# A graph-network kernel: the second message matrix folded into the update's, degrees counted in an attention pass, the update's base made ahead, and four smaller moves

## The chip, the cores and the metric

One core of one Trainium2 chip runs the whole program in one launch. The metric is the device time of an execution in microseconds (us); lower is better. TensorE is written PE, VectorE DVE, ScalarE ACT, GpSimd POOL and SyncE SP, as in the profile.

## The reference

`x` is 6250 nodes by 128; 100000 edges sorted by destination carry `src`, `dst`, 64 attributes and a weight. Every layer works on `h = relu(layernorm(x))` and adds its result to `x`.

```python
# layer 0: messages from col to row, then an MLP and a batch norm with fixed statistics
agg = segment_sum(h[col] * fsum[:, None], row)
out = softplus(agg @ Wi1 + bi1) @ Wi2 + bi2
out = gamma * (out - mov_mean) * rsqrt(mov_var + BN_EPS) + beta
# layer 1: attention with one head, twice, each followed by a residual and a layer norm
# layer 2
messages = relu(concat(x[src], edge_attr, g) @ Wm1.T + bm1) @ Wm2.T + bm2
aggregated = segment_sum(messages, dst) / maximum(degree, 1)[:, None]
delta = relu(concat(x, aggregated, g) @ Wu1.T + bu1) @ Wu2.T + bu2
out = layernorm(x + delta) * ln_g + ln_b
# layer 3: attention with 8 heads, self loops included, plus a bias
```

## The kernel before

Nodes lie in 52 tiles of 128 (`NBP`), in 13 groups of 4 (`NG`, `GN`). X, ACC, H, XI and Y hold one row per node, in SBUF. Edges lie in 832 tiles of 128 slots, worked in 104 halves of 8 tiles; `edge_records`, `onehots`, `onehots_turned` and `layer0_messages` are DRAM tensors.

**Setup** (`setup`). DVE finds the slot of each edge in 7 chunks of 112 columns. Each chunk runs `slot_round` for 25 pairs of node tiles: `equal_to`, four scans in `running_count`, `carry_on`, `mask`, `gather_slots` (L661 to L676). All of them read and write SBUF. POOL shares the first chunk. From chunk 0 on, POOL scatters the records of the finished chunks to DRAM with one indirect DMA per column (L439, 782 in all), while DVE works on the next chunk.

**Layer 0** has a pass by destination (`layer0_dst_pass`) and one by source (`layer0_src_pass`). In the latter POOL subtracts an index row from the messages' indices (L1342), ACT makes a one-hot of the difference with Abs and Relu (L1352, L1354), PE multiplies (`sum_tiles`, L1116) and DVE adds the 8 products to the node tiles (`add_sums`, L1129), whose places it first loads into registers (`node_tiles`, L1089). Rings of 4 one-hots and 8 message buffers tie them together. `softplus_product` follows; its `after0` multiplies by `bn_scale` (L1787), adds to X (L1788) and counts statistics (L179).

**A node product** (`node_product`) goes through the 13 groups: ACT normalises 4 tiles into XI (L1741), PE turns them (L896), ACT copies them out of PSUM (L947), PE multiplies (L922), DVE takes the result (`take_product`), SP stores the table. With two sources and `w2` it is the update of layer 2: PE turns both (L896), adds both products in PSUM (L905), ACT applies Relu (L960), PE multiplies by `wu2T` (L920), DVE adds `bu2` (L1861), adds XI (L1862) and counts statistics (L1864).

**Attention** (`gat_pass`): POOL gathers rows with 832 indirect DMAs (L1389), PE picks and sums, DVE adds sums. Before the first gather POOL reduces a maximum over partitions (L1481). `mlp_pass` is layer 2's pass over edges; it sums relu(...) rows with a column of ones, the degree. Then `degree2` divides (L1841 to L1844), a node product with `wm2T` gives the mean message (L1849, L1854), and the update follows. `norm_into_x` normalises and adds into X.

All engines meet at the end of each block. The order within a block is written by hand and held by semaphores; each engine runs its own list in order.

## Time and profile before

| what | us |
|---|---|
| median of 3 runs | 7350.69 (7348.01 to 7358.4) |
| profiled execution, its own time | 7349.52 |
| its span | 7347.5 |

| stretch | us | PE busy | DVE busy | ACT busy | POOL busy | PE clock |
|---|---|---|---|---|---|---|
| setup, 0 to 1252 | 1252 | 107 | 777 | 160 | 848 | 0.58 |
| layer 0 by destination, to 2349 | 1097 | 507 | 332 | 220 | 809 | 0.66 |
| layer 0 by source, to 2623 | 274 | 215 | 188 | 238 | 199 | 0.98 |
| softplus product, first table, to 2744 | 121 | 71 | 75 | 58 | 0 | 0.72 |
| attention pass 0, to 3804 | 1060 | 502 | 347 | 297 | 786 | 0.58 |
| second table, to 3876 | 72 | 23 | 58 | 30 | 0 | 0.71 |
| attention pass 1, to 4928 | 1052 | 500 | 355 | 297 | 785 | 0.59 |
| norms and layer 2's table, to 5022 | 94 | 22 | 68 | 49 | 0 | 0.64 |
| layer 2 over edges, to 6075 | 1053 | 805 | 380 | 239 | 785 | 0.68 |
| layer 2's update, norm, layer 3's table, to 6234 | 159 | 96 | 107 | 76 | 0 | 0.82 |
| attention pass with 8 heads, to 7322 | 1088 | 491 | 528 | 73 | 787 | 0.66 |
| last rows and store | 25.5 | 0 | 18 | 0 | 0 | 0.50 |

Busy times are those of the profiled execution; an engine's sum is below the span because it waits. The clock is the granted share of 2.4 GHz, a mean over the stretch: 0.50 is 1.2 GHz throughout. Register and semaphore instructions and the issue of DMAs are not busy time, except POOL's indirect DMAs, whose rows are the time POOL makes descriptors.

### The profile page before, as it was taken

What the parts mean: (1) busy time and instruction counts of PE and PEld (TensorE: products, weight loads), DVE (VectorE), ACT (ScalarE), POOL (GpSimd) and SP (SyncE); (2) the same over time, 40 slices, a digit from 0 to 9 for tenths busy, and PEclk for the clock granted to TensorE, in tenths of its full rate; (3) what the DMA queues carried; (4) which work ended last, traced back from release to release, by engine and by line L of the source; (5) the groups of instructions that cost most, each with busy time, mean ns of one, the idle gap of its engine ahead of it and who ended that gap; (6) DMA issues with size and microseconds to landing.
All of it is one profiled execution on the core that took longest, in us unless ns stands there. A gap on an engine that the chain in (4) does not pass through costs nothing. (4 is left out here: it accounts for less than half of the span.)

```text
span 7347.5 us, 89302 instructions
## 1 busy us (share of the span) xinstructions
PE 3339.2 (45%) x17325; PEld 2965.8 (40%) x17326; DVE 3231.2 (44%) x10135; ACT 1737.8 (24%) x4276; POOL 4999.3 (68%) x5176
## 2 busy tenths in 40 slices
PE   5000000444444854444444444436777775444443
PEld 2000000444444744444433444435767674344443
DVE  8777711322333663333344333344333336544445
ACT  7000000222123852222232222223222224000000
POOL 2777776777777717777746777754777770777775
PEclk9555555666666975555556565556666667666666
DMA  6233332444444624444424444433444441444443
GB/s 230 92 111 104 105 118 85 160 155 155 156 157 146 211 65 136 130 134 130 130 84 140 131 133 131 130 91 117 136 134 134 135 124 34 133 133 132 132 131 106
DMA packets 507457, 942.53 MB, mean 128 GB/s; under 512 B 204299, under 2 KB 240635, under 8 KB 507256
## 3 DMA queue, kind: packets, MB, share of 16 engines
q1 hardware_dynamic: 349240, 637.41, 26.1%
q0 software_dynamic: 158144, 304.31, 15.9%
q8 instruction: 26, 0.43, 0.0%
q14 instruction: 47, 0.39, 0.0%
HBM read 673.90 MB, written 270.84 MB: 129 GB/s over the span
## 5 line engine op out<-in xcount | busy, mean ns | idle before, releaser
L1389 POOL DMA_INDIRECT edge_buf<-node_table,ixr x1664 | 1571.8, 945 | 618.8 <-issue 507.0
L1389 POOL DMA_INDIRECT Y<-node_table,ixr x1664 | 1569.6, 943 | 519.3 <-issue 518.4
L1129 DVE TENSOR_TENSOR ACC<-ACC,bank 128x129 f32 (+2 forms) x3744 | 1090.6, 291 | 1096.3 <-PE bank L1116 468.4
L1556 PE MATMUL bank<-adc,turned_buf 128*128 x2496 | 340.2, 195 | 1476.7 <-issue 591.5
L1297 POOL DMA_INDIRECT layer_messages<-edge_buf,ixr x832 | 809.3, 973 | 291.4 <-issue 263.3
L439 POOL DMA_INDIRECT edge_records<-edge_buf x782 | 790.7, 1011 | 255.1 <-issue 246.9
L1556 PEld LDWEIGHTS bank<-adc,turned_buf 128*128 128x128 bf16 x2496 | 257.1, 103 | 1606.2 <-issue 1552.1
L1116 PE MATMUL bank<-edge_buf,Y 128*128 128x129 f32 (+2 forms) x3744 | 821.9, 406 | 143.3 <-ACT edge_buf L1542 98.8
L1116 PE MATMUL bank<-Y 128*128 128x129 f32 (+1 forms) x3328 | 770.1, 423 | 160.4 <-ACT Y L1542 91.5
L1116 PEld LDWEIGHTS bank<-edge_buf,Y 128*128 128x128 f32 x3744 | 765.3, 309 | 174.1 <-DVE ACC L1129 136.9
L1116 PEld LDWEIGHTS bank<-Y 128*128 128x128 f32 x3328 | 720.0, 325 | 183.6 <-issue 87.7
L1504 DVE TENSOR_REDUCE pk<-bank 128x16 f32<-128x48 f32 (+1 forms) x312 | 100.2, 321 | 1006.9 <-DMA Y<-node_table,ixr 505.3
L1245 PE MATMUL bank<-ident,Y 128*128 128x128 f32 x832 | 204.3, 427 | 729.7 <-DVE Y L1082 727.4
L1245 PEld LDWEIGHTS bank<-ident,Y 128*128 128x128 f32 x832 | 163.2, 223 | 752.7 <-issue 563.4
L1675 PE MATMUL bank<-wmbT,turned_buf 64*128 64x128 f32 x1664 | 287.0, 340 | 181.1 <-DVE edge_buf L1614 90.7
L1675 PEld LDWEIGHTS bank<-wmbT,turned_buf 64*128 64x128 f32 x1664 | 260.5, 243 | 214.4 <-issue 200.3
L488 PE MATMUL bank<-Y,H 128*128 128x2 f32 (+1 forms) x6 | 1.4, 358 | 740.0 <-DVEq L735 740.0
L1257 PE MATMUL bank<-H,Y 128*128 x1664 | 323.8, 377 | 2.6 <-DVEq L1207 2.6
L1257 PEld LDWEIGHTS bank<-H,Y 128*128 128x128 f32 x1664 | 323.2, 297 | 2.8 <-issue 2.8
L1285 ACT COPY Y<-bank 128x512 f32<-128x512 f32 x208 | 123.8, 595 | 840.5 <-PE bank L1257 840.1
L1195 DVE COPY edge_buf<-XI 128x8 f32 (+1 forms) x104 | 18.4, 177 | 664.6 <-DMA layer_messages<-edge_buf,ixr 664.6
L488 PEld LDWEIGHTS bank<-Y,H 128*128 128x128 f32 x6 | 1.4, 325 | 740.2 <-issue 740.2
(284 smaller groups left out, 5309.1 us busy)
## 6 DMA issues: line engine op xcount, KB each, us to landing
Y<-onehots SPq DMA_DIRECT2D x416, 512.0 KB, 3.7
turned_buf<-onehots_turned SPq DMA_DIRECT2D x312, 256.0 KB
edge_buf<-edge_records SPq DMA_DIRECT2D x208, 288.0 KB, 2.9
layer_messages<-ACC SPq DMA_DIRECT2D x26, 2112.0 KB
onehots<-Y SPq DMA_DIRECT2D x104, 512.0 KB, 2.6
XI<-layer_messages SPq DMA_DIRECT2D x78, 528.0 KB, 4.4
edge_records<-XI SPq DMA_DIRECT2D x1, 29952.0 KB
onehots_turned<-turned_buf SPq DMA_DIRECT2D x104, 256.0 KB
```

The costliest lines, as they stand in the source:

```text
L439: pool.indirect_dma_start(rec_d, bass.IndirectOffsetOnAxis(ap=ixs[h][:, j:j + 1], axis=0), rec[h][:, j, :], None, bounds_check=SLOTS - 1, ...
L1116: ins = nc.tensor.matmul(places.at(q, j, w), tiles_of_half(onehots)[:, j, :], messages[:, j, 0:w], start=True, stop=True)
L1129: nc.vector.tensor_tensor(acc, acc, places.at(q, j, w), ALU.add).then_inc(added, 1)
L1195: nc.vector.tensor_copy(rows[h][:, :, D:D + 1], fields[:, bass.ds(t, G), R_SLOC - EA:R_SLOC - EA + 1]) \
L1245: ins = nc.tensor.transpose(bank[j // 4][:, (j % 4) * P:(j % 4) * P + P], tiles_of_half(oh[h])[:, j, :], ident[:, :])
L1257: ins = nc.tensor.matmul(bank[2 + j // 4][:, (j % 4) * P:(j % 4) * P + P], ohT[h][:, j * P:j * P + P], Hflat[:, bass.ds(at[j] * AW, D)], s ...
L1285: nc.scalar.copy(ohT[h][:, at], bank[n][:, :]).then_inc(ohT_ready, 1)
L1297: pool.indirect_dma_start(msg_d, bass.IndirectOffsetOnAxis(ap=ixr[h][:, j:j + 1], axis=0), rows[h][:, j, 0:MW], None, bounds_check=SLOTS - ...
L1389: pool.indirect_dma_start(ring[q][:, j, 0:w], None, table, bass.IndirectOffsetOnAxis(ap=ixr[q][:, j:j + 1], axis=0)).then_inc(rows_in[q], 16)
L1504: st.then(nc.vector.tensor_reduce(ps, picks(q).rearrange("p (j t k) -> p j k t", j=G, t=3), AX.X, ALU.add))
L1556: ins = nc.tensor.matmul(picks(q)[:, j * 6 * heads:(j + 1) * 6 * heads], ohbT[q][:, j * P:j * P + P], adc[:, bass.ds(at[j] * (6 * heads), ...
L1675: ins = nc.tensor.matmul(bank[2 + j // 4][:, (j % 4) * P:(j % 4) * P + P], attrT[q % 2][:, j * P:j * P + P], wmbT[:, :], start=True, stop= ...
```

## The change

1. **Layer 2.** `wm2T` is folded: setup multiplies `wubT` with `wm2` into `wmuT`, and `bm2` into the row `cmu_row`. Degrees are counted in attention pass 1: a column of ones in each buffer makes its sums 130 wide; `end1` derives `inv_deg` and `has_edge` there. `has_edge` is turned to a row, out to DRAM and back to one partition of Y (`flag_row`) within `norm_into_x`. The node product of layer 2's table gets a second product per group, `Base`: `wuaT` on the same turned rows plus `cmu_row` times the flags, which DVE takes into H with `cu_col`. The table is built in ACC. `beside2` adds `bu2` to XI. `degree2` and the product with `wm2T` are gone; `update_product` replaces the two-source one.
2. **Copies on DVE.** Node products that normalise on ACT and have no `before` (three of four) copy their turned tiles on DVE.
3. **Setup's counts in PSUM.** In chunks 1 to 6 the running counts lie in PSUM banks 2 and 3, and the scans' second operand, which they bypass, in bank 1.
4. **Layer 0 by source.** Places are loaded for two halves at a time; every eighth one-hot is made by DVE in one instruction; POOL runs one reduction over partitions at the end of its list there.
5. `bn_scale` is multiplied into `Wi2` in setup; `after0` adds straight to X.

```diff
+            cums_psum = [bank[2 + h][:, 0:2 * CH].rearrange("p (q c) -> p q c", q=2) for h in range(2)]
+            unread = bank[1][:, 0:CH]
...
-                                    work(h, eqs[h], cums[h], bass.ds(i * 2 + h, 1))
+                                    work(h, eqs[h], running[h], bass.ds(i * 2 + h, 1))
...
-                                    v.tensor_tensor_scan(cum[:, q, :], eq[:, q, :], eq[:, q, :], offs[0:EP, q, b],
-                                                         ALU.add, ALU.bypass).then_inc(count, 1)
+                                    v.tensor_tensor_scan(cum[:, q, :], eq[:, q, :], eq[:, q, :] if helped else unread,
+                                                         offs[0:EP, q, b], ALU.add, ALU.bypass).then_inc(count, 1)
...
+                        nc.tensor.matmul(bank[6][:, P:2 * P], wm2, wubT[:, :], start=True, stop=True)
+                        nc.tensor.matmul(bank[7][0:1, P:2 * P], bm2_col[:, :], wubT[:, :], start=True, stop=True)
...
+            dve_copies = normed is not None and before is None
...
+                        if dve_copies and g + 1 < NG:
+                            copy(g + 1)
                         take_product(dve, v, then, g, prod, taken, cols, after)
+                        if second:
+                            dve.wait_ge(second_done, g + 1)
+                            second.take(v, g).then_inc(second_taken, 1)
...
+        def update_product(src, w1, base, w2, before, after):
...
+                    def add_base(g):
+                        dve.wait_ge(in_hid, g + 1)
+                        v.tensor_tensor(of_group(g), of_group(g), bank[2 + g % 2][:, :], ALU.add).then_inc(z_ready, 1)
+                    prepare(0)
+                    prepare(1)
+                    add_base(0)
+                    for g in range(NG):
+                        if g + 2 < NG:
+                            prepare(g + 2)
                         if g + 1 < NG:
-                            copy(g + 1)
+                            add_base(g + 1)
+                        take_product(dve, v, then, g, prod, taken, D, after)
...
-                tiles[0:1, bass.ds(n * G, G)], engines=[engine], min_val=0,
+                tiles[0:1, bass.ds(n * G, halves * G)], engines=[engine], min_val=0,
...
+                    nc.gpsimd.memset(gmax[:, :], 0.0).then_inc(gmax_set, 1)
+                    pool.wait_ge(gmax_set, 1)
+                    pool.partition_all_reduce(gmax_all[:, :], gmax[:, :], P, bass.bass_isa.ReduceOp.max).then_inc(gmax_set, 1)
+                    pool.wait_ge(gmax_set, 2)
...
+                    def onehot_here(i, q):
+
+                        dve.wait_ge(msg_in[q], i * 16 + 16)
+                        dve.wait_ge(summed, i * deep + q - oh_deep + 1)
+                        nc.vector.tensor_tensor(tiles_of_half(onehots[q]), bank[0][:, 0:P].unsqueeze(1).to_broadcast([P, G, P]),
+                                                by_tile[q][:, :, D:D + 1].to_broadcast([P, G, P]), ALU.is_equal) \
+                            .then_inc(oh_ready[q], 1)
+
+                    def body(i, first):
+                        for pair in range(deep // 2):
+                            n = i * deep + 2 * pair
+                            at = node_tiles(mybir.EngineType.DVE, acc_of_s, n, 2)
+                            for k in range(2):
+                                add_to(dve, n + k, 2 * pair + k, two_sets, sums, at[k * G:k * G + G], D, summed, n + k + 1, added)
+                            if 2 * pair + 1 == by_vector - oh_deep:
+                                onehot_here(i, by_vector)
...
-                then(v.tensor_tensor(ACC[:, at, 0:D], rows_psum, columns(bn_scale, 2), ALU.mult))
-                then(v.tensor_tensor(X[:, at, :], X[:, at, :], ACC[:, at, 0:D], ALU.add))
+                then(v.tensor_tensor(X[:, at, :], X[:, at, :], rows_psum, ALU.add))
...
+                    if l == 1:
+                        deg = ACC[:, :, D + 1:D + 2]
+                        then(v.tensor_scalar(inv_deg[:, :].unsqueeze(2), deg, 1.0, None, ALU.max))
+                        then(v.reciprocal(inv_deg[:, :], inv_deg[:, :]))
+                        then(v.tensor_tensor(has_edge[:, :].unsqueeze(2), deg, inv_deg[:, :].unsqueeze(2), ALU.mult))
...
+                def product(g, turned):
+                    o = bank[2 + g % 2][:, :]
+                    nc.tensor.matmul(o, wuaT[:, :], turned, start=True, stop=False)
+                    return nc.tensor.matmul(o, cmu_row[:, :], flag_row[:, Base.at(g)], start=False, stop=True)
...
-            node_product([XI], [wmaT], after_h, normed=relu_norm_x, store=(tab_d[2], H, D))
+            node_product(XI, wmaT, after_h, normed=relu_norm_x, store=(tab_d[2], ACC, D), second=Base)
...
+                add_row(v, then, XI, vec["L2_gnn_bu2"][0])
...
-                then(v.tensor_tensor(ACC[:, at, 0:D], rows_psum, columns(vec["L2_gnn_bu2"][0], 2), ALU.add))
-                then(v.tensor_tensor(H[:, at, 0:D], ACC[:, at, 0:D], XI[:, at, :], ALU.add))
+                then(v.tensor_tensor(Y[:, at, :], rows_psum, XI[:, at, :], ALU.add))
...
-            node_product([XI, Y], [wuaT, wubT], after_u, w2=wu2T, bias=cu_col)
+            update_product(ACC, wmuT, update_base, wu2T, mean2, after_u)
```

PE's list where layer 2's table is made, from its first group on, before and now: `wmaT` makes the table, `ident` turns.

```order
L896 MATMUL bank<-ident,XI 128x128 x8
L922 MATMUL bank<-wmaT,edge_buf 128x128 x4
L896 MATMUL bank<-ident,XI 128x128 x4
L922 MATMUL bank<-wmaT,edge_buf 128x128 x4
L896 MATMUL bank<-ident,XI 128x128 x4
```

```order
L912 MATMUL bank<-ident,XI 128x128 x8
L1979 MATMUL bank<-edge_buf,wuaT 128x512
L1980 MATMUL bank<-Y,cmu_row 128x512
L926 MATMUL bank<-wmaT,edge_buf 128x128 x4
L912 MATMUL bank<-ident,XI 128x128 x4
```

Two products of 512 columns now stand ahead of the table's four in each of the 13 groups.

PE's list in layer 2's update, before (its first group and most of the second) and now.

```order
L896 MATMUL bank<-ident,XI 128x128 x4
L896 MATMUL bank<-ident,Y 128x128 x4
L905 MATMUL bank<-edge_buf,wuaT 128x512
L905 MATMUL bank<-edge_buf,wubT 128x512
L896 MATMUL bank<-ident,XI 128x128 x4
L896 MATMUL bank<-ident,Y 128x128 x4
L920 MATMUL bank<-wu2T,edge_buf 128x128 x4
```

```order
L993 MATMUL bank<-ident,ACC 128x128 x8
L1000 MATMUL bank<-edge_buf,wmuT 128x512
L993 MATMUL bank<-ident,ACC 128x128 x4
L1000 MATMUL bank<-edge_buf,wmuT 128x512
L1007 MATMUL bank<-wu2T,edge_buf 128x128 x4
L993 MATMUL bank<-ident,ACC 128x128 x4
```

Per group four turns and one product of 512 columns went, and the product for the next group now stands ahead of the last four.

POOL's list between the pass by source and the first attention pass, before and now; the bare ISA row loads the code that the reduction needs.

```order
L1342 TENSOR_TENSOR Y<-iota_row,edge_buf 128x1024
L88 REGISTER_ALU
L88 COMPARE_AND_BRANCH
L1318 UNCONDITIONAL_BRANCH
L105 ISA
L1478 UNCONDITIONAL_BRANCH
L1481 ISA
L1481 ISA gmax_all<-gmax 128x1
L1389 DMA edge_buf<-node_table,ixr_115 128x129 x8
```

```order
L1432 MEMSET gmax 128x8
L1434 ISA
L1434 ISA gmax_all<-gmax 128x8
L1404 UNCONDITIONAL_BRANCH
L105 ISA
L1585 UNCONDITIONAL_BRANCH
L1588 ISA gmax_all<-gmax 128x1
L1496 DMA edge_buf<-node_table,ixr_118 128x129 x8
```

The bare ISA row moved from the start of the attention pass to the end of the pass by source.

## Rows read from the trace of the kernel before

**Rows 1.** The page, part 1: busy time, share of the span, instructions.
```profile
PE 3339.2 (45%) x17325; PEld 2965.8 (40%) x17326; DVE 3231.2 (44%) x10135; ACT 1737.8 (24%) x4276; POOL 4999.3 (68%) x5176
```
**Rows 2.** The page, part 5: groups; busy us, mean ns, idle before, releaser.
```profile
L1389 POOL DMA_INDIRECT Y<-node_table,ixr x1664 | 1569.6, 943 | 519.3 <-issue 518.4
L1297 POOL DMA_INDIRECT layer_messages<-edge_buf,ixr x832 | 809.3, 973 | 291.4 <-issue 263.3
```
**Rows 3.** Stretches: length, busy us (count) of each engine, PE clock, DMA share.
```profile
204.00:928.00 724.00, 0.00 (x0) 0.00 (x0) 566.89 (x1875) 13.63 (x76) 553.56 (x542) 0.50 0.33 108
...
2351.00:2623.00 272.00, 215.43 (x1664) 196.15 (x1664) 185.77 (x833) 237.76 (x208) 198.78 (x104) 0.98 0.65 204
2667.00:2706.00 39.00, 22.99 (x91) 19.77 (x89) 34.98 (x105) 0.00 (x0) 0.00 (x0) 0.50 0.00 0
...
4990.00:5020.00 30.00, 22.20 (x156) 19.21 (x156) 11.04 (x26) 26.45 (x65) 0.00 (x0) 0.89 0.34 100
...
6109.00:6162.00 53.00, 49.32 (x253) 33.10 (x252) 34.47 (x104) 21.23 (x39) 0.00 (x0) 0.97 0.00 1
```
**Rows 4.** Groups, POOL, 204 to 928 us (DVE counts slots beside it).
```profile
L439 POOL DMA_INDIRECT edge_records<-edge_buf x542 | 554.3, 1023 | 179.0 <-issue 174.5 <-DMA edge_buf<-in_edge_attr_dram 4.6
```
**Rows 5.** Timeline, setup: start us, us, engine, line.
```profile
401.37 0.39 DVE L673 TENSOR_TENSOR XI<-XI,Y 128x224 f32<-128x224 f32 x1
401.46 1.14 POOL L439 DMA_INDIRECT edge_records<-edge_buf  x1 [0.30 <-issue]
...
402.20 0.82 DVE L676 TENSOR_TENSOR XI<-XI 128x224 f32 x2
402.91 0.97 POOL L439 DMA_INDIRECT edge_records<-edge_buf  x1 [0.30 <-issue]
```
**Rows 6.** Groups, DVE alone, 2359 to 2623 us (layer 0 by source).
```profile
L1129 DVE TENSOR_TENSOR ACC<-ACC,bank 128x128 f32 x416 | 119.7, 288 | 86.0 <-DVE H L1129 66.3 <-issue 13.8 <-PE bank L1116 5.9
```
**Rows 7.** Line L1089: duration ns min/median/max, first and last start.
```profile
L1089 DVEq TENSOR_LOAD <-acc_of_s x104: 593/598/850, 2354.8 to 2620.2; - x104
```
**Rows 8.** Groups, whole span: a one-hot on DVE.
```profile
L1082 DVE TENSOR_TENSOR Y<-bank,XI 128x1024 f32<-128x1024 f32 x104 | 127.3, 1224 | 11.8 <-DVE XI L1183 9.9
```
**Rows 9.** Timeline, start of attention pass 0 and of pass 1.
```profile
2752.02 0.38 POOL L1481 PARTITION_ALL_REDUCE gmax_all<-gmax  x1 [139.93 <-issue]
...
3876.04 0.39 POOL L1481 PARTITION_ALL_REDUCE gmax_all<-gmax  x1 [84.96 <-DVEq L1429]
```
**Rows 10.** Groups, 2667 to 2706 us (`after0`).
```profile
L1788 DVE TENSOR_TENSOR X<-X,ACC 128x256 f32<-128x256 f32 x26 | 11.0, 425 | 0.9
L1787 DVE TENSOR_TENSOR ACC<-bank,bn_scale 128x256 f32<-128x256 f32 x26 | 11.0, 424 | 2.2
```
**Rows 11.** Groups, 4990 to 5020 us (layer 2's table).
```profile
L1741 ACT ACTIVATE XI<-X,shift,var 128x128 f32<-128x128 f32 x52 | 21.5, 501 | 2.0 <-PEq L106 2.0
...
L947 ACT COPY edge_buf<-bank 128x512 f32<-128x512 f32 x13 | 7.6, 584 | 0.3 <-PE bank L896 0.3
```
**Rows 12.** Timeline, one group of layer 2's update, PE at full clock.
```profile
6133.59 1.09 PE L905 MATMUL bank<-edge_buf,wuaT 128*128 128x512 f32 x2
6133.80 0.42 DVE L1862 TENSOR_TENSOR H<-ACC,XI 128x256 f32<-128x256 f32 x1
6134.26 0.49 DVE L1864 BATCH_NORM_STATS2 stats<-H 128x6 f32<-128x128 f32 x2
6134.78 0.42 DVE L1861 TENSOR_TENSOR ACC<-bank,L_gnn_bu 128x256 f32<-128x256 f32 x1
6135.38 0.60 PE L896 MATMUL bank<-ident,XI 128*128 128x128 f32 x4
6136.32 1.05 PE L920 MATMUL bank<-wu2T,edge_buf 128*128 128x128 f32 x7
```
**Rows 13.** Groups: 128x512 on DVE, out of SBUF (`mean2`) and out of PSUM.
```profile
L1849 DVE TENSOR_TENSOR ACC<-ACC,mean 128x512 f32<-128x512 f32 x13 | 9.0, 691 | 2.3 <-DVE Y L1854 1.4 <-PEq L788 0.5
...
L990 DVE TENSOR_SCALAR XI<-bank,bi_col 128x512 f32<-128x512 f32 x13 | 9.8, 751 | 6.7 <-PE bank L1019 6.0
```

More of the change, by code:

```diff
@@ L928, in _ @@
                     for g in range(NG):
-                        if w2 is not None:
-                            first(g)
                         if g + 1 < NG:
@@ L951, in _ @@
                             normed(g).then_inc(norm_done, 1)
-                    copy(0)
+                    if not dve_copies:
+                        copy(0)
                     for g in range(NG):
@@ L1316, in layer0_src_pass @@
             rounds = HALVES // deep
+            by_vector = deep - 1
             with nc.Block() as block:
@@ L1705, in after, with add_row @@
                 then(v.tensor_copy(ad[:, at, :], rows_psum[:, :, D + heads:cols]))
-            node_product([XI], [wx[l]], after, before, normed, cols=cols, store=(table, H, D + heads))
-        def add_row_to_x(v, then, row):
+            node_product(XI, wx[l], after, before, normed, cols=cols, store=(table, H, D + heads))
+        def add_row(v, then, t, row):
             in_psum = bank[7][:, 0:D]
             then(v.tensor_copy(in_psum, row[:, :]))
-            then(v.tensor_tensor(X[:, :, :], X[:, :, :], per_col(in_psum), ALU.add))
+            then(v.tensor_tensor(t[:, :, :], t[:, :, :], per_col(in_psum), ALU.add))
         def self_loops(v, then, heads):
```

263 lines of the change are left out of this document (168 added, 95 removed).

## The prediction

> **What bounds the kernel.** I read the page's first part for the engines, its groups for the costliest work, then stretches, and inside each stretch the groups, the releasers and a piece of timeline. POOL is busy 68% of the span, more than any other [rows 1], and its indirect DMAs go at a fixed pace: 943 ns for a gather, 973 ns for a scatter, with 0.3 us between two that nobody but POOL's own issue fills [rows 2, 5]. Six long stretches (setup's scatter, layer 0 by destination, three attention passes, layer 2 over edges) are such lists. There DVE, ACT and PE may gain or lose a little and nothing moves. The change leaves the number of gathers and scatters as it is. What it can win lies in the pace of setup's scatter, in the start of attention pass 0, and in the short stretches where POOL isn't the bound: layer 0 by source and the node products.
>
> **The change, term by term.**
>
> *Counts in PSUM (setup).* From 204 to 928 us DVE counts slots while POOL scatters. POOL's 542 scatters there take 1023 ns each [rows 4], those of layer 0, beside other DVE work, 973 [rows 2]. The timeline shows why: the scatter at 401.46 begins while `mask`, which reads two SBUF tensors, is running, and takes 1.14 us; it ends later by what `mask` had left. The scatter at 402.91 begins behind the last `gather_slots` by start and takes 0.97 [rows 5]. So a scatter waits where a DVE instruction with two SBUF inputs is already under way. The change gives the scans, `mask` and `gather_slots` one SBUF input each. In the stretches of layer 0 DVE's instructions are of that kind, and the pace there is the floor. Gain: 542 x (1023 - 973) = 27 us; I take 26, as a few instructions with two SBUF inputs stay in `slot_rows`. POOL must stay the bound for that. DVE needs 724 / 6 = 121 us per chunk [rows 3]; POOL's 112 scatters need 112 x (0.973 + 0.30) = 143 us, and 148 now. DVE has 22 us to spare. Setup's additions (two small products, two copies, one multiply) lie before the scatter's end and cost nothing while it lasts.
>
> Against this stands a rule. The rows show no price for PSUM: 424 ns out of PSUM, 425 ns out of SBUF for 128x256 [rows 10]. The Trainium skill (VectorE: DVE Perf Modes, the section on the TRN2 errata) gives VectorE a fixed 58 cycles out of SBUF and 120 out of PSUM, 0.065 us more at 0.96 GHz. By it, as an estimate, the 250 instructions of a chunk that touch the counts would add 16 us, DVE would stand at 137 us, and the sum would be the same with 6 us of margin left.
>
> *Layer 0 by source.* In 272 us DVE is busy 186 and idle 86 [rows 3, 6]; ACT is busy 238, PE 215, POOL 199. The idle time isn't a lack of work: before each half DVE's sequencer loads eight places, 598 ns [rows 7], and cannot issue an add meanwhile. That is 104 times about 0.73 us with what stands around it. DVE is the bound, ACT is next. Now 52 loads of sixteen places take their place. If a load is a fixed price, 52 x (0.73 - 0.09) = 33 us go; the 0.09 is the register work that stays between two halves. DVE gets 13 one-hots of 1.22 us [rows 8], each hiding the load behind it, so 13 x (1.22 + 0.06 - 0.73) = 7 us come back. Gain 26 us. The others then need, of (272 - 26) / 13 = 18.9 us per eight halves: ACT 7/8 x 238 / 13 = 16.0, PE 16.6, POOL 13.4. None is the new bound, but ACT is near. What I don't have is the price of sixteen places. Its bounds: 0.6 us (nothing per place) and 1.2 us (twice eight). I take 0.6, since 0.6 for one place or eight is what a round trip looks like, and keep 1.2 as a rival.
>
> *The reduction's code.* Pass 0 begins at 2744, and its reduction starts at 2752.02, behind nothing but POOL's own issue; pass 1 begins at 3876, and its reduction starts at 3876.04 [rows 9]. The two stretches differ by the same 8 us (1060 and 1052 in the table of stretches). Now the load stands at the end of POOL's list by source. POOL's last one-hot there ends about 10 us before DVE's last add (four halves of 2.6 us, the depth of the ring), and load and reduction take 8. Gain 8 us; if the cover is short, the next block starts some us later and the gain shrinks.
>
> *`after0`.* 26 times one instruction of 424 ns and the 0.03 us to the next. DVE is busy 35 of 39 us [rows 3, 10]. Gain 26 x 0.458 = 12 us. PE at half clock is busy 23 of the 27 us that stay, so it isn't the bound.
>
> *Copies on DVE.* ACT has 21.5 us of norms and 7.6 of copies in 30 [rows 3, 11]. Without copies it needs 1.65 us per group; the group takes 26.45 / 13 = 2.03 us now [rows 3]. DVE with its copy of about 0.7 [rows 13] and two takes of about 0.55 (0.42 and a short copy, an estimate from rows 12) needs about 1.85. Two tables gain 2.4 and 1.2 us, 3.5 together.
>
> *Degrees.* Three small instructions in `end1`, +1 us. Columns 130 instead of 129 and the memsets lie beside POOL's gathers. The flags' way through DRAM lies beside 13 groups of norm work. `add_row` on XI (7 us on DVE) lies beside POOL's first four halves of gathers, 32 x 1.25 = 40 us, which need nothing of DVE. All cost nothing as long as POOL is the bound there.
>
> *The base, made ahead.* Layer 2's table took 30 us, bound by ACT. PE now has per group four turns, eight short and four long matrix instructions. From one group of the old update: four long ones take 6135.38 - 6133.59 = 1.79 us, eight turns 0.94, eight short ones about 1.0 [rows 12]. That is 0.47 + 1.0 + 1.79 = 3.25 us, against ACT's 1.65 and DVE's 0.7 + 2 x 0.46 + 0.75 = 2.4. PE is the bound: 13 x 3.25 = 42, and 4 to fill and empty. Cost 46 - 30 = +16 us.
>
> *The update.* From the end of layer 2's edges at 6075 to 6162 us stand `degree2`, the product with `wm2T` and the update, 87 us; the update is bound by PE, busy 49 of 53 [rows 3]. Now DVE has per group `mean2` 0.69 with 0.15 around it, the base 0.72, and two takes of 0.46 + 0.52 [rows 12, 13]: 3.55 us, against PE's 0.47 + 0.90 + 1.0 = 2.4. DVE is the bound: 13 x 3.55 = 46, and 5 for the chain of the first group, where PE still has half clock. 51 instead of 87: gain 35 us (36 less the add's wait).
>
> **Sum.** -26 - 26 - 8 - 12 - 3.5 + 1 + 16 - 35 = -93.5 us. The profiled execution took 7349.5 (its span 7347.5 and 2.0 around it), so 7256; the median of the runs is 1.2 above it: 7257 us.
>
> **Rivals.**
> *A load of sixteen costs twice that of eight.* 39 of 52 loads are not hidden: 39 x 0.6 = 23 us come back, total 7280. For it: nothing in the trace has another size. The Trainium skill has both answers. DMA: Bandwidth & Descriptors (Latency and other measured facts) calls 600 ns a floor of the load, which speaks for my price; Runtime: NRT & Kernel Launch (Instruction fetch mechanics) gives about 200 ns per register from HBM. By the second, eight would take 1.6 us; the trace's 0.6 denies it here. Chance 0.15.
> *Setup's scatter isn't freed* because something else of DVE (its writes, or the comparison in SBUF) delays it: 26 us stay, 7283. Against it stands layer 0's pace. Chance 0.10.
> *PE stays at half clock* in the two rebuilt stretches, as it did all through `after0` at 0.50 [rows 3]. Then the table needs 13 x 6.5 + 4 = 89 us and the update 13 x 4.7 + 5 = 66, 58 us more: 7315. Against it: the old table and update, with PE less or as busy, ran at 0.89 and 0.97. Chance 0.06.
> *The first two together*, 7306: 0.02.
> *Slower than before*: DVE becomes setup's bound. If the counts in PSUM made each of a chunk's 250 instructions slower, DVE would pass POOL at 22 / 250 = 0.09 us each. From there every further us of a chunk counts six times. The kernel is slower by over 0.2% when 67.5 us of other gains and 15 more are eaten, 83 / 6 = 14 us per chunk above the 148 of now, which is 41 us in all or 0.165 us per instruction; total 7366 and up. Against it: 424 beside 425 ns [rows 10]. For it: no row has a scan in PSUM. Chance 0.03.
> The forecast keeps 0.64.
>
> **Numbers.** My case alone spans 7240 (every term at its full size, a smaller fill) to 7273 (ACT eats a part by source, PE fills slowly). The first two rivals at 7280 and 7283 must be in, with their own spread: 7238 to 7292. That leaves out the third to fifth rival, 0.11, and some 0.05 of the tails. 0.2%, 15 us, is what a measurement can tell from no change. Every case but the last is faster by more: faster 0.96, same 0.01, slower 0.03.
>
> **What would show it.** Right: scatters in setup at 973 ns beside DVE, setup shorter by about 26 us; layer 0 by source near 246 us with loads near 0.6 us; no wait of 8 us at the first reduction; layer 2's table at 46 us with PE without a gap; the update at 51 us with DVE without a gap. Wrong: loads of 1.2 us, or DVE idle on one-hots of ACT; scatters still at 1023 ns; PE's clock near 0.5 in the table or the update; DVE chunks over 143 us.

## The result, and the profile after

The changed kernel takes 7312.08 us (7307.35 to 7317.1, five runs) where before takes 7350.69 (7346.68 to 7358.4, five runs): ratio 0.9948, 95% interval 0.9933 to 0.9962. The sign is the forecast's, the size is not: 38.6 us gained instead of 93.5, and the time lies above the range of 7238 to 7292. The profiled executions differ by 32.1 us of span (7347.5 and 7315.4); the profiled one after is the slowest of its five. What follows is between these two.

Stretches of the changed kernel, cut at the events that cut the table of before. Columns: length, busy us and count of PE, PEld, DVE, ACT, POOL, PE's clock, DMA share, GB/s; the last three lines are pieces of layer 2's table and of `after0`.

```profile
0.00:1225.40 1225.40, 113.05 (x298) 51.43 (x299) 782.56 (x2480) 160.58 (x360) 821.42 (x909) 0.58 0.37 122
1225.40:2320.90 1095.50, 511.75 (x2496) 487.89 (x2496) 331.53 (x632) 219.60 (x417) 809.30 (x832) 0.66 0.44 151
2320.90:2587.00 266.10, 201.75 (x1664) 191.93 (x1664) 204.10 (x848) 204.51 (x182) 172.80 (x93) 0.98 0.67 211
...
6051.00:6128.50 77.50, 48.10 (x182) 32.94 (x182) 41.17 (x104) 16.99 (x26) 0.00 (x0) 0.74 0.00 1
...
2631.00:2658.00 27.00, 15.43 (x89) 13.28 (x88) 23.68 (x79) 0.00 (x0) 0.00 (x0) 0.82 0.00 0
...
4938.00:4961.00 23.00, 22.02 (x57) 12.60 (x58) 6.88 (x13) 18.96 (x50) 0.00 (x0) 0.50 0.08 23
4961.00:4996.50 35.50, 33.51 (x152) 18.15 (x151) 21.86 (x40) 0.00 (x0) 0.00 (x0) 1.00 0.26 78
```

They answer to [rows 3]. Stage by stage, forecast and measured:

| term | forecast | measured |
|---|---|---|
| setup | -26 | -27 (1252 to 1225) |
| layer 0 by source | -26 | -8 (274 to 266) |
| the reduction's code | -8 | -7 (pass 0: 1060 to 1053) |
| `after0` | -12 | -12 (39 to 27) |
| copies on DVE | -3.5 | -1 (table 0 in 28.5, was 28.8; layer 3's table in 26.8, was 27.4) |
| degrees | +1 | +1 |
| the base made ahead | +16 | +31 (layer 2's table 27 to 58; the forecast counted the old one as 30) |
| the update | -35 | -10 (87 to 77) |

Layer 0 by destination gives 1 us, and the 8-head pass takes 2 us more, a spread that the experiments show between equal programs too. With these the column adds up to -32, as the span says. Three terms carry the error: 18 us by source, 15 in layer 2's table, 25 in the update.

**By source**, the loads of places on the line of the loads (duration ns, least, median, largest; first and last start):

```profile
L1168 DVEq TENSOR_LOAD <-acc_of_d x416: 593/598/633, 2719.1 to 7280.7; - x139
...
L1168 DVEq TENSOR_LOAD <-acc_of_s x52: 1096/1100/1359, 2327.1 to 2581.7; - x52
```

A load of eight takes 598 ns as in [rows 7], one of sixteen 1100. The timeline shows what it costs where no one-hot covers it, and where one does:

```profile
2450.32 0.29 DVE L1211 TENSOR_TENSOR ACC<-ACC,bank 128x128 f32 x1 [1.66 <-issue]
...
2453.54 0.29 DVE L1211 TENSOR_TENSOR H<-H,bank 128x128 f32 x1
2455.07 0.29 DVE L1211 TENSOR_TENSOR ACC<-ACC,bank 128x128 f32 x1 [1.24 <-PE bank L1195]
...
2458.30 0.29 DVE L1211 TENSOR_TENSOR H<-H,bank 128x128 f32 x1
2458.58 1.22 DVE L1460 TENSOR_TENSOR Y<-bank,edge_buf 128x1024 f32<-128x1024 f32 x1
...
2460.11 0.29 DVE L1211 TENSOR_TENSOR ACC<-ACC,bank 128x128 f32 x1 [0.30 <-issue]
```

DVE idles 1.66 us before the add that follows an open load where its list starts another turn of the loop, and 1.24 us at most of the others. The profile names PE's product there, but that had ended at 2454.18, while the load ran from 2453.67 to 2454.77. With a one-hot, DVE's last add ends at 2458.59 and the next begins at 2460.11, 1.52 us later: the one-hot hides the load, but takes longer than most of the gaps that it fills, and saves nothing.

**Layer 2's table** runs at half clock until 4961, though PE is busy without a gap from 4942 on. One group at half clock, and one at full:

```profile
4947.58 1.92 PE L1979 MATMUL bank<-edge_buf,wuaT 128*128 128x512 f32 x2
4949.42 2.07 PE L1980 MATMUL bank<-Y,cmu_row 1*128 1x512 f32 x2
4951.42 2.08 PE L926 MATMUL bank<-wmaT,edge_buf 128*128 128x128 f32 x8
4953.29 1.06 PE L912 MATMUL bank<-ident,XI 128*128 128x128 f32 x4
...
4964.29 1.02 PE L1979 MATMUL bank<-edge_buf,wuaT 128*128 128x512 f32 x2
4965.24 1.12 PE L1980 MATMUL bank<-Y,cmu_row 1*128 1x512 f32 x2
4966.29 1.16 PE L926 MATMUL bank<-wmaT,edge_buf 128*128 128x128 f32 x8
4967.29 0.60 PE L912 MATMUL bank<-ident,XI 128*128 128x128 f32 x4
```

A group takes 4954.14 - 4947.58 = 6.56 us at half clock (the next L1979 begins at 4954.14) and 4967.73 - 4964.29 = 3.44 at full. Three groups fall in the slow part: about 3 x 3.1 = 9 us, and more with the start.

**The update**: one group of the changed kernel.

```profile
6099.96 0.69 DVE L1995 TENSOR_TENSOR ACC<-ACC,inv_deg 128x512 f32<-128x512 f32 x1 [0.15 <-DVE stats L183]
6100.76 0.50 PEld L993 LDWEIGHTS bank<-ident,ACC 128*128 128x128 f32 x4 [2.66 <-DVEq L971]
6100.76 0.90 PE L993 MATMUL bank<-ident,ACC 128*128 128x128 f32 x4 [2.47 <-DVEq L971]
...
6101.45 1.92 PE L1000 MATMUL bank<-edge_buf,wmuT 128*128 128x512 f32 x2
...
6103.41 0.69 DVE L975 TENSOR_TENSOR H<-H,bank 128x512 f32<-128x512 f32 x1 [2.76 <-PE bank L1000]
...
6104.26 0.42 DVE L2000 TENSOR_TENSOR Y<-bank,XI 128x256 f32<-128x256 f32 x1 [0.17 <-PE bank L1007]
```

Read it as a ring. DVE scales group g+2 (L1995); PE turns it (L993), since its list has these turns ahead of the first product of g+1 (L1000); DVE's add of the base (L975) waits 2.76 us for that product; then come the takes of g, and PE waits 2.47 us for the next scaling. DVE and PE work in turns, 6.3 us a group, and neither is the bound. The clock, in the same place:

```profile
6093.50:6097.50 4.00, 3.25 (x9) 2.22 (x10) 1.03 (x2) 0.59 (x1) 0.00 (x0) 0.59 0.00 0
6097.50:6101.00 3.50, 1.03 (x8) 0.84 (x8) 2.81 (x8) 0.72 (x1) 0.00 (x0) 0.98 0.00 0
6101.00:6104.50 3.50, 3.50 (x13) 2.47 (x12) 0.93 (x2) 0.96 (x2) 0.00 (x0) 0.51 0.00 0
```

It is full while PE mostly waits (busy 1.03 of 3.5 us) and half while PE works. The Trainium skill (TensorE: Matmul & The Clock Gate, the section on how the clock gate's oscillation bites in real kernels) describes work in bursts, with waits for DMA between, that meets the low clock each time; the trace shows the same with waits for DVE.

### The profile page after: what moved, and what is told of

It reads as the page before. It is cut to its first block and busy times, and to the rows that moved or that the text cites. A ratio compares the mean times of both kernels' runs of the same rounds, so it can differ in the third digit from the quotient of the medians.

```text
span 7315.4 us, 88637 instructions
## 1 busy us (share of the span) xinstructions
PE 3315.1 (45%) x17147; PEld 2929.7 (40%) x17148; DVE 3264.7 (45%) x10122; ACT 1673.6 (23%) x4184; POOL 4946.4 (68%) x5165
## 5 line engine op out<-in xcount | busy, mean ns | idle before, releaser
L1211 DVE TENSOR_TENSOR ACC<-ACC,bank 128x129 f32 (+3 forms) x3744 | 1091.4, 291 | 1077.1 <-PE bank L1195 502.4
L445 POOL DMA_INDIRECT edge_records<-edge_buf x782 | 763.7, 977 | 255.3 <-issue 243.5
L1195 PE MATMUL bank<-edge_buf,Y 128*128 128x129 f32 (+3 forms) x3744 | 812.9, 404 | 150.1 <-ACT edge_buf L1649 98.6
L1195 PE MATMUL bank<-Y 128*128 128x129 f32 (+2 forms) x3328 | 759.4, 418 | 164.3 <-ACT Y L1649 91.8
```

Source lines behind the costliest of these rows:

```text
L445: pool.indirect_dma_start(rec_d, bass.IndirectOffsetOnAxis(ap=ixs[h][:, j:j + 1], axis=0), rec[h][:, j, :], None, bounds_check=SLOTS - 1, ...
L1195: ins = nc.tensor.matmul(places.at(q, j, w), tiles_of_half(onehots)[:, j, :], messages[:, j, 0:w], start=True, stop=True)
L1211: nc.vector.tensor_tensor(acc, acc, places.at(q, j, w), ALU.add).then_inc(added, 1)
```

## The experiments

Each is an edit of the changed kernel. For the tables and the update the times are from the first turn or the last add before it to the last take; the changed kernel itself has 56.4 us for layer 2's table and 77.0 for the update.

**1. The order of the update.**

```diff
                     for g in range(NG):
+                        if g + 1 < NG:
+                            first(g + 1)
                         if g + 2 < NG:
                             turn(g + 2)
-                        if g + 1 < NG:
-                            first(g + 1)
                         last(g)
```

> Only the order of PE's work in the update is other: each group's first product is issued ahead of the turns of the group behind it. Theory A (in the changed kernel DVE and PE wait for each other in a ring: take, scale, turn, first product, add; 6.3 us per group): now the add of the base needs nothing of the group just scaled, DVE's own 3.55 us per group is the bound, the update takes 13 x 3.55 + 5 = 51 us instead of 77.5, and the kernel gains 26 us, to about 7286. Theory B (the loss is PE's clock alone, which each burst of the changed kernel meets at its lower level): the order changes nothing that matters, the first product stays at 1.9 us and the update within 5 us of 77.

Measured: 7294.22 us (7290.9 to 7294.83, four runs), ratio to before 0.9921 (0.9905 to 0.9938). The update takes 54.0 us (6052.1 to 6106.1), 23 less; 51 and a gain of 26 were expected. By the medians the kernel gains 18 us on the changed one, by the spans of the profiled executions 23: that of the changed kernel is the slowest of its five.

```profile
6080.07 1.07 PE L1000 MATMUL bank<-edge_buf,wmuT 128*128 128x512 f32 x2
...
6081.90 0.69 DVE L1995 TENSOR_TENSOR ACC<-ACC,inv_deg 128x512 f32<-128x512 f32 x1 [0.15 <-DVE stats L183]
...
6082.74 0.69 DVE L975 TENSOR_TENSOR H<-H,bank 128x512 f32<-128x512 f32 x1
...
6083.20 1.06 PE L1007 MATMUL bank<-wu2T,edge_buf 128*128 128x128 f32 x8
...
6083.85 0.42 DVE L2000 TENSOR_TENSOR Y<-bank,XI 128x256 f32<-128x256 f32 x1 [0.42 <-PE bank L1007]
```

The first product is done before DVE scales, and the add of the base follows at once. A group takes 4.03 us (one first product at 6080.07, the next at 6084.10). The clock is 0.99 from 6058 on, although nothing was done for it: it rose with the ring cut. Theory A, then. How much of the 23 us is the ring's and how much the clock's, the run doesn't part. The 0.42 us left in front of the take is the same fault once more: the last product stands behind turns that wait for the scaling. Experiment 8 moves them too.

**2. The table without the one-row product.**

```diff
-                    nc.tensor.matmul(o, wuaT[:, :], turned, start=True, stop=False)
-                    return nc.tensor.matmul(o, cmu_row[:, :], flag_row[:, Base.at(g)], start=False, stop=True)
+                    return nc.tensor.matmul(o, wuaT[:, :], turned, start=True, stop=True)
```

> The one-row product (weights 1x128, flags 1x512) is left out of layer 2's table, and with it the term of bm2 for nodes that have an edge. A group then needs 3.44 - 1.12 = 2.32 us of PE at full clock and 6.57 - 2.0 = 4.6 at half. Theory A (the one-row product is also what keeps PE at half clock for the table's first 22 us, though PE is busy without a gap there): the clock rises within 6 us of the first turn, as in the other tables, and the table takes 1 x 4.6 + 12 x 2.32 + 3 = 36 us instead of 58. Theory B (the rise comes late for another reason, such as the length of the pause before): half clock for 22 us again, 4.6 groups in it, then 8.4 x 2.32, with 2 to empty: 44 us.

Measured, in one execution: the table takes 33.4 us (4940.3 to 4973.7).

```profile
4940.00:4945.50 5.50, 4.80 (x16) 3.37 (x16) 1.38 (x2) 5.50 (x15) 0.00 (x0) 0.50 0.00 0
4945.50:4974.00 28.50, 27.40 (x168) 20.85 (x167) 25.72 (x50) 13.20 (x35) 0.00 (x0) 0.99 0.37 111
```

The clock is up 5 us after the first turn instead of 22. Of the 23 us, 13 x 1.12 = 15 are the product's own time at full clock; the rest is the earlier rise. Theory A, as far as it goes: this run changes the product's length and its rows at once.

**3. The same product on all rows.** Rows or length?

```diff
-                    return nc.tensor.matmul(o, cmu_row[:, :], flag_row[:, Base.at(g)], start=False, stop=True)
+                    return nc.tensor.matmul(o, wubT[:, :], turned, start=False, stop=True)
```

> In layer 2's table the one-row product is replaced by a product of the same shape at PE's output, 128x512 fp32, but with all 128 rows of weights and data (wubT and the turned nodes; the base is then another number than the reference's). PE's time stays the same: 6.57 us per group at half clock, 3.44 at full. Theory A (a product that fills one row of PE hardly counts as work for the clock): the clock rises within 6 us of the first turn, and the table takes 1 x 6.57 + 12 x 3.44 + 3 = 51 us instead of 56.4. Theory B (the late rise has to do with long products, or with the start of this stretch): half clock for 22 us again, 56 us.

Measured, in one execution: 43.0 us (4943.1 to 4986.1).

```profile
4943.00:4949.00 6.00, 5.45 (x18) 3.42 (x19) 1.38 (x2) 6.00 (x17) 0.00 (x0) 0.60 0.00 0
4949.00:4987.00 38.00, 36.58 (x193) 24.91 (x191) 27.35 (x50) 12.53 (x33) 0.00 (x0) 1.00 0.28 83
```

Same amount of output, and the clock is up after 5 us: theory A. With the product's time kept, it was its single row that held the clock down. It is also shorter than I expected (51). A group at full clock takes 4964.97 - 4961.92 = 3.05 us, not 3.44, and the weight loads come earlier. Ahead of this product and ahead of L926 PEld idles 0.24 us, ahead of the one-row product, and of the one behind it, 0.76:

```profile
4962.35 0.19 PEld L1980 LDWEIGHTS bank<-edge_buf,wubT 128*128 128x128 f32 x1 [0.24 <-issue]
```

and in the changed kernel

```profile
4965.24 0.29 PEld L1980 LDWEIGHTS bank<-Y,cmu_row 1*128 1x128 f32 x2 [0.76 <-issue]
```

**4. The clock warmed up ahead of the table.** Twelve, then eighteen products of 128x512 in the norms before it, unread; all else as in the changed kernel. The edit with twelve:

```diff
+                        pe.wait_ge(norm_done, 9)
+                        for n in range(12):
+                            nc.tensor.matmul(bank[6][:, :], ident[:, :], ACC[:, 0:GN, 0:D], start=True, stop=True)
```

> PE gets 12 products of 128x512 fp32, whose result nobody reads, in the last 15 us of the norms ahead of layer 2's table; all else as in the changed kernel. Theory A (only the cold start costs): the clock is at its upper level at the first turn and stays there, and the table takes 13 x 3.44 + 2 = 47 us instead of 58. Theory B (the one-row product pulls the clock down): the clock falls to 0.50 again in the first groups and the table takes 53 us or more.

Measured, in one execution: 53.3 us (4940.8 to 4994.1). The clock was full from 4923, PE idle from 4931, the clock half at 4938, and it came back at about 4956. So the run doesn't tell the theories apart; the level was lost before the table began.

> As warm_table, with 18 unread products instead of 12, so that PE works up to the table's start; in warm_table they ended at 4931, the clock fell at about 4937, and the first turn at 4941 met half clock. The one-row product stays. Theory A (the one-row product holds the clock down whatever stood before it): the clock is full at the first turn, falls to 0.50 within the first two groups, and the table still takes 50 us or more from the first turn to the last take. Theory B (only the start decides): full clock throughout, 13 x 3.44 = 45 us.

Measured, in one execution: 50.1 us (4941.0 to 4991.1). PE ended at about 4936.3.

```profile
4937.00:4939.00 2.00, 0.00 (x0) 0.00 (x0) 0.69 (x2) 0.28 (x1) 0.00 (x0) 1.00 0.00 0
4939.00:4941.00 2.00, 0.00 (x1) 0.01 (x1) 0.00 (x0) 1.71 (x5) 0.00 (x0) 0.73 0.00 0
4941.00:4950.00 9.00, 8.58 (x24) 5.17 (x25) 2.23 (x4) 9.00 (x24) 0.00 (x0) 0.50 0.00 0
4950.00:4992.00 42.00, 40.61 (x185) 22.22 (x184) 26.47 (x48) 9.40 (x25) 0.00 (x0) 1.00 0.26 76
```

The level was lost in the pause of 4.7 us between the last unread product and the first turn. Again neither theory is met at the first turn. What the runs add is that with the one-row product the rise is not only late but varies, also where nothing near the table was changed. From the first turn to the rise it is 22 us in the changed kernel, update_order (experiment 1) and loads_small (experiment 6), and the table takes 56.4 or 56.5 us; it is 16 us in hot_back (experiment 7) and in the two runs on setup's scatters, counts_sbuf and scan_sbuf, and the table takes 53.3. The warm_table run, with 15.9 and 53.3, is one of these, so its unread products gained nothing that shows. Only warm_long, with 9 and 50.1, is quicker, and one run can't tell whether the warming did it. All eight runs with the one-row fp32 product took 9 us or more, the five without it (no_flags, full_rows, flags_bf16 and the two of experiment 8) 4 to 6.

**5. The flags in bf16.** The bias row is cut in three bf16 parts that add up to it; one pass of three rows takes the place of the fp32 product.

```diff
-    flag_d = dram("edge_flags", [NBP, P])
+    flag_d = dram("edge_flags", [NBP, P], BF16)
...
-                    return nc.tensor.matmul(o, cmu_row[:, :], flag_row[:, Base.at(g)], start=False, stop=True)
+                    return nc.tensor.matmul(o, cmu_rows[:, :], flag_row[:, Base.at(g)], start=False, stop=True)
```

> The one-row fp32 product of layer 2's table becomes one of three rows in bf16 (the row of Wm2's bias cut in three bf16 parts that add up to it, the flags 0 or 1 three times), one pass in place of fp32's. By the run without the product the table takes 33.4 us from the first turn to the last take, with it 56.4. Theory A (its time and its hold on the clock both go by how long it runs): about a quarter of 1.12 us per group, clock up within 8 us, the table at 33.4 + 13 x 0.3 = 37 us, the kernel 19 us faster than the changed one. Theory B (any product of few rows keeps the clock down): half clock for 20 us or more, 45 us or more.

Measured: 7301.74 us (7300.58 to 7303.13, four runs), ratio to before 0.993 (0.9914 to 0.9947). The table takes 38.2 us (4944.0 to 4982.2), 18 less than in the changed kernel and 15 less than in the three runs that had 53.3. The kernel gains 10 us by the medians, 13 by the ratios to before, where 19 were expected. The timeline has the new product at

```profile
4975.23 0.39 PE L1996 MATMUL bank<-Y,cmu_rows 3*128 3x512 bf16 x1
```

and the stretches up to and from the clock's rise:

```profile
4943.90:4949.00 5.10, 4.60 (x15) 2.55 (x16) 1.38 (x2) 5.10 (x15) 0.00 (x0) 0.59 0.00 0
4949.00:4983.00 34.00, 32.67 (x182) 20.66 (x181) 27.26 (x50) 13.39 (x35) 0.00 (x0) 1.00 0.31 93
```

Theory A: 0.39 us instead of 1.12, and the clock is up after 4 us, though three rows are few too. A product of few rows need not hold the clock down, then, where it is short. Cutting the row in parts on DVE put 0.3 us in front of the table (66.3 us from attention pass 1's last add to the first turn, 66.0 in the changed kernel); in experiment 8 that is done in setup.

**6. Loads of other sizes, by source.** Per pair of halves 4 + 4 and 2 + 6 places. `some_tiles` is a load of `count` places from `at` on.

```diff
-                            at = node_tiles(mybir.EngineType.DVE, acc_of_s, n, 2)
-                            for k in range(2):
-                                add_to(dve, n + k, 2 * pair + k, two_sets, sums, at[k * G:k * G + G], D, summed, n + k + 1, added)
+                            for k, first_load in enumerate((4, 2)):
+                                at = list(some_tiles(acc_of_s, (n + k) * G, first_load))
+                                at += list(some_tiles(acc_of_s, (n + k) * G + first_load, G - first_load))
+                                add_to(dve, n + k, 2 * pair + k, two_sets, sums, at, D, summed, n + k + 1, added)
```

> Layer 0 by source, DVE's loads of places: per pair of halves 4 + 4 and 2 + 6 places in four loads instead of one of sixteen; nothing else. Theory A (about 0.1 us per load and 0.063 per place, drawn from 598 ns for eight and 1100 for sixteen): 0.22, 0.35, 0.47 us for 2, 4 and 6 places, together 1.4 us per pair instead of 1.1, and with a little for each more issue the stretch takes some 10 to 20 us more than 266. Theory B (0.6 us is a floor up to eight places): all four 0.6, 2.4 us per pair, the stretch 50 us longer.

Measured, in one execution: 7414.37 us; the adds by source take 354.0 us (2333.0 to 2687.0) where the changed kernel's take 254.5, 99 more. One load of four, one of two, one of six:

```profile
L1175 DVEq TENSOR_LOAD <-acc_of_s x1: 341/341/341, 2433.3 to 2433.3; - x1
...
L1175 DVEq TENSOR_LOAD <-acc_of_s x1: 534/534/534, 2435.6 to 2435.6; - x1
...
L1175 DVEq TENSOR_LOAD <-acc_of_s x1: 1408/1408/1408, 2436.3 to 2436.3; - x1
```

Four, eight and sixteen places take 341, 598 and 1100 ns: (1100 - 598) / 8 = 0.063 us per place and about 0.09 fixed. There is no floor at 0.6, and theory B falls. But two and six take 534 and 1408: (1408 - 534) / 4 = 0.22 us per place. I expected neither. These two pay about 3.5 times as much per place. Neither count is a multiple of four; the load of six also starts two places past one, and no run here parts count and start, but the load of two starts where others do. The Trainium skill has both numbers: DMA: Bandwidth & Descriptors (Latency and other measured facts) gives 600 ns as a floor, which the 341 ns here denies; Runtime: NRT & Kernel Launch (Instruction fetch mechanics) gives some 200 ns per register, which is near the 0.22 us between two and six places and not near four, eight or sixteen. The sum fits: 341 + 341 + 534 + 1408 = 2.62 us a pair and three more issues at some 0.1, less 1.10, is 1.8 us, and 52 x 1.8 = 94.

**7. DVE's one-hots given back.**

```diff
-            by_vector = deep - 1
+            by_vector = deep
...
-                            if 2 * pair + 1 == by_vector - oh_deep:
-                                onehot_here(i, by_vector)
```

> Layer 0 by source with DVE's 13 one-hots given back to POOL and ACT; loads stay at sixteen places. Theory A (DVE stays the bound; its one-hot stands where a visible load of 1.10 us would stand, and the step between two pairs takes 1.52 us with it and 1.66 without): the stretch grows by 13 x 0.14 = 2 us at most, ACT's 104 x 2.3 = 239 us being still below 266. Theory B (ACT was the bound of the old stretch, and freeing it brought the 8 us that were gained): the stretch returns to 274 us.

Measured, in one execution: the adds take 252.5 us (2333.1 to 2585.6), 2 less than with them. DVE is the bound either way, and its one-hots earn nothing. Theory A, with the sign of the 2 us turned: the expectation took 1.66 us for every step without a one-hot, but where the one-hots stood DVE now idles 1.33 us (as before 2460.09), against 1.52 with them, and 13 x 0.19 = 2.5.

**Setup's scatters**, two runs. First the counts back in SBUF, the scans' unread second input staying in PSUM:

```diff
-                            running = cums if helped else cums_psum
+                            running = cums
```

> DVE's running counts in setup go back from PSUM to SBUF, nothing else. Theory A (a scatter waits where a DVE instruction that reads two SBUF tensors is under way): the scatters beside them take 1023 ns again instead of 972, and setup is 26 to 28 us longer. Theory B (the scatters got shorter for another reason, such as the unread second input of the scans): they stay near 975 ns and setup within 5 us.

Then the other way round:

```diff
-                                    v.tensor_tensor_scan(cum[:, q, :], eq[:, q, :], eq[:, q, :] if helped else unread,
+                                    v.tensor_tensor_scan(cum[:, q, :], eq[:, q, :], eq[:, q, :],
```

> Counts stay in PSUM; only the scans' second input, which they don't use, is the comparison in SBUF again in place of a row in PSUM. With the counts back in SBUF the scatters stayed at 975 ns, against what was expected: none of the 150 that began while a scan ran was delayed, and the 52 that began while the mask ran found only 0.12 us of it left. Theory A (a scatter waits for what is left of any DVE instruction with two SBUF inputs, and the scans were the ones that mattered once the two lists had fallen into step): the scatters that begin in a scan's first half take 1.05 to 1.12 us again, the mean is 985 ns or more, and setup grows by 5 us or more. Theory B (scans never delayed a scatter, the mask and the order of the lists do): 972 to 976 ns and no change.

Measured, one execution each, POOL's scatters from 206 to 928 us (busy, mean ns, idle before), first with the counts in SBUF, then with the scans' second input in SBUF:

```profile
L445 POOL DMA_INDIRECT edge_records<-edge_buf x560 | 545.8, 975 | 176.6 <-issue 168.7 <-DMA edge_buf<-in_edge_attr_dram 7.9
```

```profile
L445 POOL DMA_INDIRECT edge_records<-edge_buf x553 | 548.6, 992 | 174.2 <-issue 166.0 <-DMA edge_buf<-in_edge_attr_dram 8.2
```

The first result goes against what I expected (1023): with the scans' second input in PSUM, moving the counts back costs nothing that shows. The second meets theory A: 86 of the 156 scatters that began while a scan ran took over 1050 ns, the mean is 992, and the first add by source comes 10 us later than in the other runs of that chip (2345.0 against 2334.3). In before, all but one of the 77 scatters that began in a mask and 75 of the 148 that began in a scan were over 1050 ns. In the run with counts in SBUF the mask still reads two SBUF tensors and 52 scatters began in it; only 2 were over 1050, since most found no more than 0.14 us of it left, where those of before found 0.30. Both lists repeat themselves, so they fall into step, and the step decides what a scatter meets. The Trainium skill (SBUF — State Buffer, SBUF: two separate sides) calls the port that VectorE and GpSimd share an exclusive lock that an instruction with two SBUF inputs holds to its end; the runs agree with that, and show besides that the sum of such instructions says little. The mean was 1023 ns in before, 992 with the counts alone in PSUM, 975 with the scans' second input alone in PSUM and 972 with both: the second alone wins nearly all of the 27 us, the first alone some 17 of them, and they don't add up.

**8. The edits that helped, together.** PE's order `first(g + 1)`, `last(g)`, `turn(g + 2)`; the flags in bf16, the parts made in setup; the one-hots given back.

```diff
...
+                        if g + 1 < NG:
+                            first(g + 1)
+                        last(g)
                         if g + 2 < NG:
                             turn(g + 2)
-                        if g + 1 < NG:
-                            first(g + 1)
-                        last(g)
...
```

> Three edits together: in the update PE issues the first product of the next group, then the last product of this one, then the turns; layer 2's table has the flags' product in bf16 with three rows (the parts of the bias row made in setup); DVE's one-hots by source go back to POOL and ACT. If they add up: update 13 x 3.6 + 5 = 52 us instead of 77 (in update_order, where the last product still stood behind the turns, 54), table 38 instead of 56, by source 2 less. Sum -25 - 18 - 2 = -45 to the changed kernel, about 7267 where before takes 7350. The other way (the edits meet in the same wait, or the flags' three more transfers delay the table): 7285 or more.

Measured: 7267.8 us (7267.38 to 7268.89, four runs) where before has 7350.13 in the same comparison: ratio 0.9888 (0.9871 to 0.9904). The update takes 48.5 us (6032.6 to 6081.1), the table 38.7 (4938.0 to 4976.7), the adds by source 252.3: 28.5, 17.7 and 2.2 less than in the changed kernel, 48.4 in sum, and the spans differ by 7315.4 - 7266.9 = 48.5. By the medians it is 44 us less than the changed kernel, of 45 expected. The edits add up. DVE in the update:

```profile
6049.82 0.69 DVE L983 TENSOR_TENSOR H<-H,bank 128x512 f32<-128x512 f32 x1
...
6050.43 0.42 DVE L2009 TENSOR_TENSOR Y<-bank,XI 128x256 f32<-128x256 f32 x1
...
6053.34 0.69 DVE L983 TENSOR_TENSOR H<-H,bank 128x512 f32<-128x512 f32 x1
```

3.52 us per group (6049.82 to 6053.34), against the 3.55 that the prediction had for DVE as the bound.

> best3 with the 18 unread products ahead of layer 2's table. Theory A (with the short product the clock, once up, stays up, and the first groups gain): the table 3 us shorter than best3's (about 1.5 groups at 3 us less each), less up to 1 us if the products end late; 7264. Theory B (the clock falls in the pause between the stages however short): the same as best3, or up to 2 us slower.

Measured: 7267.62 us (7267.01 to 7269.47, four runs), the same as best3. The unread products ended at 4932, the clock had fallen to half by the first turn at 4937.3, and the table takes 38.5 us. Theory B.

## Why the prediction was right and wrong

- **Setup, right in size, half right in its reason.** 27 us for 26. The step that named "the scans, `mask` and `gather_slots`" together was too coarse. In before none of the 77 scatters that began in a `gather_slots` was over 1050 ns. Freeing the scans does nearly all of it; the counts in PSUM do over half of it alone and add nothing that these runs can show once the scans are free. The timeline at 401.46 [rows 5] showed a true wait, but which instruction a scatter meets is a matter of step between two lists. DVE did not become the bound: the scans with their result in PSUM take 442 ns where they took 438, 4 ns more, where the slower rival needed 165. The Trainium skill (VectorE: DVE Perf Modes, the TRN2 errata) has 62 cycles more out of PSUM than out of SBUF, by an estimate 0.065 us, which isn't seen here.
- **By source, the term that I knew to be open.** The forecast took 0.6 us for sixteen places and kept 1.2 as a rival worth 23 us. 1.10 was measured: 39 x 0.5 = 19.5 us come back, and 18 are missing. Failed step: "0.6 for one place or eight is what a round trip looks like"; four places took 0.34. One price seen at one size can't tell a fixed cost from a slope. The chance of 0.15 was too low: the trace had nothing against it.
- **Reduction's code, `after0`, degrees, right**: -7, -12, +1. In `after0` PE's clock is 0.82 where it had 0.50 [rows 3].
- **Copies on DVE**: the pace in table 0 is as worked out, 1.83 us per group (L1808's takes, every group from 2674.36 on) against 1.85; but the second and third take, behind groups at half clock, come 1.3 us later than before and eat most of the 2 us. The term had no line for the start.
- **The base, +31 for +16.** Failed step: "That is 0.47 + 1.0 + 1.79 = 3.25 us", times thirteen, at full clock throughout. 3.44 was measured at full clock (right within 6%), but 6.56 in the first 22 us, while the one-row product kept the clock at half (experiments 2 to 5). The rival "PE stays at half clock" was there, with 0.06, and half of it came true. That its total, 7315, lies near the measured time is luck: it added 43 us for the table and 15 for the update, and knew nothing of the loads. I let the old table's 0.89 speak for the new one, whose PE work is of another kind.
- **The update, -10 for -35.** Failed step: "DVE is the bound: 13 x 3.55". The maximum over engines holds only where each engine can run ahead of the others, and I had added up lists without following one group through them. PE's list has turn(g + 2) ahead of first(g + 1), and DVE's has the scaling of g + 2 ahead of the add for g + 1; so the add waits for a chain through PE that begins with DVE's own last step. The rows of before could give all its links: 0.69 + 0.15, then 0.47, 1.09, 0.69, then two takes of 0.98 = 5.1 us per group, 66 in all, at full clock. So by that estimate the ring alone is 15 us over my 51, and the half clock, at which PE worked in it, the other 11 up to 77. Experiments 1 and 8 show that the order is the cause of both: with the ring cut the update takes 54.0 and 48.5, and the clock looks after itself. DVE's list was right: its terms add up to 3.52 us (3.55 in the prediction is a slip of 0.4 us in all), and 3.52 is what experiment 8 has.

In sum the three failed steps are 18 + 15 + 25 = 58 of the 61 us by which the spans miss the forecast, and the copies most of the other 3. With the two that can be mended mended (table and update), the kernel stands at 7268, 11 us above the forecast, of which 18 are the loads.

## What to carry to other kernels

Before taking the busiest engine as the bound of a stage with several engines in step, follow one group through every engine's list: where the wait of engine A stands behind work that needs engine A's own previous step, the period is the sum around that ring, and a reordering of two lines in one list can be worth more than the work removed. A matrix product of one row was not a small product here: in fp32 it took as long as one of 128 rows, the weight loads around it came later, and PE's clock stayed down; in bf16 parts it cost a third. And where one size has been timed, the price of twice the size is open: put both ends in the range and don't give one of them four fifths.

## What the runs showed of the hardware

- Register loads on DVE's queue, from SBUF: 341, 598 and 1100 ns for four, eight and sixteen places, but 534 for two and 1408 for six.
- With a one-row fp32 product taking a third of PE's time the clock stayed at 0.50 for 22 us in three runs, 16 in four and 9 in one, although PE was busy with hardly a gap; with the same product on 128 rows it was at 1.00 after 5, and with three bf16 rows after 4 to 5.
- Bursts in the wrong rhythm meet the clock in the wrong phase: 0.51 and 0.59 while PE worked, 0.98 while it waited, group after group, in a ring of 6.3 us.
- The full clock didn't outlast pauses of 4.7 us (warm_long) and about 5 us (best3_warm) between the last product and the first turn.
- Weight loads ahead of and behind the one-row product began 0.76 us after the load before ended, against 0.24 between products of 128 rows.
- Of the scatters on POOL that began while a DVE scan or mask ran, 151 of 225 took over 1050 ns in before, where both inputs lie in SBUF, and none of 297 in the changed kernel, where one of the two lies in PSUM.
